# Expanded rows of the edge passes: three parts summed in one PSUM bank and copied by ScalarE, two banks for each edge layer

## The chip, the cores and the metric

The kernel runs on one core of one Trainium2 chip. The metric is the device time of one execution in microseconds. The program is one launch of about 330,000 instructions. TensorE writes to PSUM, which has eight banks of 512 f32 values in each of 128 partitions; `bank[0]` to `bank[7]` are these.

## The reference

Four graph networks run one after the other over the same 12,500 nodes (64 features) and 212,500 edges, which are sorted by destination. Between them stand a residual and a layer norm. The change touches the third, which has five layers:

```python
for l in range(5):
    h = leaky(x @ W1[l] + b1[l]) @ W2[l] + b2[l]
    e = leaky(edge_attr @ We1[l] + be1[l]) @ We2[l] + be2[l]     # 32 -> 64 -> 64, per edge
    msg = h[src] * e * dot_scale[l]
    agg = jax.ops.segment_sum(msg, dst, num_segments=n)
    x = layernorm(x + agg * res_w[l]) * ln_g[l] + ln_b[l]
```

## The kernel before

The hybrid pass does the edge part of one layer: `h[src] * e`, summed by destination. It runs five times, each with 271 *works*. A work is a batch of edges: tiles of 128 edges, one edge a partition. Two kinds alternate.

- A **near** work (147 a pass) has 7 tiles ("cells"). Its source rows are picked out of a table in SBUF by one-hot matmuls: `table_parts` holds every f32 row as three bf16 parts of 64 columns side by side (192 columns), and `hot_buf` holds the one-hot matrices in fp8, loaded by SP from DRAM, a chunk for each work. Seven near works make a strip. Its sums by destination come from one-hot matmuls too, into `bank[6]`, over the whole strip.
- A **far** work (124 a pass) has 8 tiles. Its source rows are gathered from DRAM by GpSimd, eight indirect DMAs a work (line 1133), up to four works ahead. Its one-hot matrices are made by VectorE (line 1275).

Both kinds have the two edge layers: the hidden layer (f32 matmuls of the edge attributes, line 1180, into `bank[4]`; ScalarE copies it to `hidden` with the bias, line 1145; VectorE does the leaky relu, line 1260), then the edge layer (a bias matmul, line 1188, and f32 matmuls, line 1192, into `bank[5]`). VectorE multiplies this with the source rows (lines 1285 and 1288). The product is split in three bf16 parts: ScalarE writes the high part (line 1150), VectorE takes it off (line 1313), ScalarE writes the middle part (line 1154), VectorE the low part (line 1318). TensorE adds up (lines 1217 near, 1225 far), VectorE reduces the three parts of the sum (lines 1325 and 1330) and adds them to `acc` (lines 1341 and 1350).

*Expansion before.* For a near work, `expand` runs 14 matmuls (7 cells, two sides) of 192 columns, line 1205, in two lots of four and three cells. Each lot goes to a pair of banks of a ring (`bank[0:2]`, `bank[2:4]`), 256 columns apart, and VectorE sums the three parts of each cell out of the pair into `cell_row` (`cell_sums`, line 1268). The far sums take a turn in the same ring. `s_free` counts what VectorE has emptied, and the numbers `op`, `ring`, `filled` and `added` of a work say which turn of the ring is its own.

*Order.* Each engine has its order written out as a `turn` per work, unrolled over 26 works inside a loop. Per work n, TensorE does: the hidden layer of n + 3, `expand` of n + 2 (if near), the edge layer of n + 2, `add_up` of n. VectorE does, one work ahead of TensorE (n its newest product): `take_sums` of n - 2, `multiply` of n, `cell_sums` part 0 or `one_hot` of n + 1, `rest_of_high` of n, `leaky` of n + 2, `cell_sums` part 1, `low_part` of n, `add_sums_of` n - 2. With one bank for each edge layer, the hidden layer waits until ScalarE has copied the one before, and the edge layer until VectorE has multiplied the one before.

## Time and profile before

| | us |
|---|---|
| median of 3 timed runs | 22706.24 (22622.63 to 22733.8) |
| the profiled execution | 22674.76 |
| its span, first to last instruction | 22672.7 |
| of that, the stretch with the five hybrid passes | about 10830 to 21170 |

The mean granted TensorE clock over the span is 0.735 of full speed. The page gives each engine's busy time; its groups say how often a line ran, how long one took and what ended the idle time ahead of it. "remote" there is a semaphore for which no instruction of the record ended at that moment; "issue" is time in which the engine waited for nothing that the profile shows. Matmul starts are those of issue, and their ends are modelled.

### The profile page before, as it was taken

The page shows a single profiled execution, that of the slowest core. Times are in us where ns is not written, and L with a number is a line of the kernel's source. Part 1 is how long each engine was busy: PE and PEld are TensorE (multiplying, and loading weights), DVE is VectorE, ACT ScalarE, POOL GpSimd, SP SyncE. Part 2 cuts the span into 40 slices and gives each one's busy share as a digit, 9 for nine tenths or more (in the row PEclk, how much of TensorE's full clock was granted, in tenths as well). Part 3 has the DMA queues.
Part 4 walks back from the last instruction along what each step waited for, and adds up shares of the span by engine and source line. Part 5 has one row for each costly group of instructions (what it writes and reads, how often), then busy time and mean ns, then how long its engine had stood idle before and what let it go on. Part 6 is the DMA issues. An engine that isn't in the chain of part 4 may idle for free. (4 is left out here: it accounts for less than half of the span.)

```text
span 22672.7 us, 329567 instructions
## 1 busy us (share of the span) xinstructions
PE 12966.2 (57%) x95507; PEld 10907.3 (48%) x95507; DVE 11406.3 (50%) x19693; ACT 5335.2 (24%) x10114; POOL 10006.5 (44%) x10482
## 2 busy tenths in 40 slices
PE   0344444556455666666566666666666666666465
PEld 0222223555345555555455555555555555555454
DVE  7544544444991121212555655565566556555413
ACT  0000000111443333333222222222222222222233
POOL 0455554665014434343455454445444544455342
PEclk9656665555557777778888887878887878778777
DMA  2111111111344434343222222222222222222343
GB/s 75 35 39 39 39 39 40 51 52 49 148 176 116 117 108 115 108 115 103 71 70 69 63 70 67 70 62 70 70 66 68 70 69 64 69 70 70 82 116 90
DMA packets 1284160, 1745.76 MB, mean 77 GB/s; under 512 B 576614, under 2 KB 828390, under 8 KB 1283174
## 3 DMA queue, kind: packets, MB, share of 16 engines
q1 hardware_dynamic: 960833, 1351.53, 19.9%
q0 software_dynamic: 317440, 348.12, 7.9%
q10 hardware_dynamic: 5040, 35.13, 0.4%
q8 instruction: 493, 8.08, 0.1%
q14 instruction: 354, 2.90, 0.0%
HBM read 1425.04 MB, written 308.76 MB: 76 GB/s over the span
## 5 line engine op out<-in xcount | busy, mean ns | idle before, releaser
L1133 POOL DMA_INDIRECT rows_buf<-feature_table,idx_buf x4960 | 4909.1, 990 | 4909.7 <-DMA idx_buf<-src_idx 3013.8
L857 POOL DMA_INDIRECT rows_buf<-feature_parts,idx_buf x2176 | 2054.4, 944 | 2878.2 <-PE banks L912 1897.8
L899 PE MATMUL banks<-sums_space,tmp 128*128 128x192 bf16 x13720 | 2090.6, 277 | 1602.1 <-issue 1109.7
L869 ACT ACTIVATE sums_space<-banks 128x384 bf16<-128x384 f32 x3920 | 1638.1, 452 | 3290.6 <-PE banks L886 2316.3
L886 PE MATMUL banks<-table_parts,tmp 128*128 128x192 bf16 x13720 | 2088.1, 276 | 299.5 <-DMA tmp<-one_hots 280.9
L899 PEld LDWEIGHTS banks<-sums_space,tmp 128*128 128x128 fp8e4 x13720 | 1333.0, 109 | 1869.2 <-issue 1831.8
L1180 PE MATMUL banks<-attr_buf,params 128*128 128x256 f32 x5420 | 1776.9, 454 | 782.9 <-ACT hidden L1145 354.6
L707 POOL DMA_INDIRECT rows_buf<-attention_table,idx_buf x1664 | 1571.9, 945 | 1455.7 <-DVE parts L1447 906.0
L1268 DVE TENSOR_REDUCE early<-banks 128x256 f32<-128x768 f32 (+1 forms) x1470 | 1253.6, 853 | 1861.9 <-remote 1482.3
L1150 ACT ACTIVATE sums_space<-onehot 128x448 bf16<-128x448 f32 (+1 forms) x1355 | 814.2, 601 | 5156.9 <-DVE onehot L1288 1442.6
L1192 PEld LDWEIGHTS banks<-params,hidden 128*128 128x128 f32 x10840 | 1768.0, 231 | 106.3 <-issue 39.0
L1192 PE MATMUL banks<-params,hidden 128*128 128x128 f32 x10840 | 1773.4, 316 | 30.0 <-issue 29.4
L1520 PE MATMUL banks<-far_ident,onehot 128*128 128x512 bf16 x1664 | 924.8, 556 | 1435.4 <-DVE red L1456 908.7
L1456 DVE TENSOR_REDUCE red<-banks 128x8 f32<-128x1024 f32 x832 | 1001.3, 1222 | 1460.8 <-remote 1194.9
L1188 PE MATMUL banks<-rest,parts 128*128 128x512 bf16 x1355 | 603.8, 446 | 1753.7 <-DVEq L1304 656.7
L1180 PEld LDWEIGHTS banks<-attr_buf,params 128*128 128x128 f32 x5420 | 1105.6, 226 | 1008.5 <-ACT hidden L1145 386.5
L886 PEld LDWEIGHTS banks<-table_parts,tmp 128*128 128x128 fp8e4 x13720 | 1412.4, 111 | 338.3 <-issue 298.4
L1205 PE MATMUL banks<-table_parts,tmp 128*128 128x192 bf16 x10290 | 1201.3, 271 | 609.1 <-issue 466.6
L1580 POOL DMA_INDIRECT edge_records<-hidden,idx_buf x1120 | 1120.6, 1001 | 717.1 <-ACT hidden L1623 378.9
L1205 PEld LDWEIGHTS banks<-table_parts,tmp 128*128 128x128 fp8e4 x10290 | 1002.3, 109 | 846.1 <-issue 733.9
L947 DVE TENSOR_REDUCE sums_space<-banks 128x64 f32<-128x192 f32 x272 | 97.2, 357 | 2575.3 <-PE banks L912 2368.8
L1217 PE MATMUL banks<-sums_space,tmp 128*128 128x192 bf16 x10290 | 1147.8, 262 | 327.0 <-issue 310.8
(380 smaller groups left out, 22377.4 us busy)
## 6 DMA issues: line engine op xcount, KB each, us to landing
tmp<-one_hots SPq DMA_DIRECT2D x1715, 448.0 KB
one_hots<-tmp SPq DMA_DIRECT2D x245, 448.0 KB
attr_buf<-attr SPq DMA_DIRECT2D x760, 128.0 KB
attr_buf<-cell_attr SPq DMA_DIRECT2D x735, 128.0 KB
rows_buf<-feature_table,idx_buf POOLq DMA_INDIRECT x4960
gathered_rows<-rows_buf SPq DMA_DIRECT2D x208, 272.0 KB
rows_buf<-gathered_rows SPq DMA_DIRECT2D x208, 272.0 KB
rows_buf<-feature_parts,idx_buf POOLq DMA_INDIRECT x2176
```

What stands on the lines that cost most here:

```text
L707: pool.indirect_dma_start(out=slot_rows(u, t), out_offset=None, in_=source, in_offset=bass.IndirectOffsetOnAxis(ap=idx_buf[:, u, t:t + 1], ...
L857: pool.indirect_dma_start(out=far_rows[:, u, t, :], out_offset=None, in_=table3, in_offset=bass.IndirectOffsetOnAxis(ap=idx_buf[:, u, t:t ...
L869: act.activation(cell_rows[:, q, 0:width], bank[q][:, 0:width], ACT.Copy).then_inc(s_cells_sb, 1)
L886: ins = pe.matmul(bank[q][:, j % 2 * 3 * D:(j % 2 + 1) * 3 * D], hot_buf[:, k, j, side * P:(side + 1) * P], table_parts[:, 2 * (k * CELLS ...
L899: ins = pe.matmul(bank[4 + h][:, half * 3 * D:(half + 1) * 3 * D], hot_buf[:, k, j, (2 + half) * P:(3 + half) * P], cell_rows[:, q, j % 2 ...
L1133: pool.indirect_dma_start(out=edge_rows[:, u, t, :], out_offset=None, in_=table, in_offset=bass.IndirectOffsetOnAxis(ap=idx_buf[:, u, t:t ...
L1180: ins = pe.matmul(bank[4][:, pair * 2 * P:(pair + 1) * 2 * P], w1[:, pair * P:(pair + 1) * P], attr_buf[:, w.attr, :, :].rearrange("p a e ...
L1192: ins = pe.matmul(bank[5][:, t * D:(t + 2) * D], hidden[:, w.side, at:at + P], w2, start=False, stop=(half == 1 and pair == 1))
L1205: ins = pe.matmul(to[:, j % 4 * 2 * P:j % 4 * 2 * P + 3 * D], hot_buf[:, w.k, j, side * P:(side + 1) * P], table_parts[:, 2 * (w.k * CELLS ...
L1217: ins = pe.matmul(bank[6][:, half * 3 * D:(half + 1) * 3 * D], hot_buf[:, w.k, j, (2 + half) * P:(3 + half) * P], sent[:, w.side, j, :], s ...
L1268: dve.tensor_reduce(out=cell_row[:, 4 * part:4 * part + cells, :], in_=pair_of_banks(w.ring + part).rearrange("p (j n) -> p j n", j=4)[:, ...
L1580: pool.indirect_dma_start(out=records, out_offset=bass.IndirectOffsetOnAxis(ap=idx_buf[:, slot, t:t + 1], axis=0), in_=record_buf[slot][:, ...
```

## The change

For a near work the expansion now writes one bank: each cell takes 64 columns of `bank[0]`, and its three parts are three matmuls of 64 columns that accumulate there, 42 matmuls for 14. ScalarE copies the 448 columns to `cell_row` in one instruction; VectorE's two reductions are gone. The ring of banks is gone too: far sums have `bank[1]`, the edge layer alternates between `bank[2]` and `bank[3]`, the hidden layer between `bank[4]` and `bank[5]`. TensorE and SP work one work further ahead with the hidden layer and its attributes, and TensorE expands before the hidden layer. VectorE multiplies first, and then takes and adds the sums of n - 2 in one go. Two semaphores, `s_row` and `s_taken`, stand for `s_free`.

```diff
 def hybrid_pass(block):
+            expanded, far_bank, strip_bank = bank[0], bank[1], bank[6]
+            def edge_bank(w):
+                return bank[2 + w.side]
+            def hidden_bank(w):
+                return bank[4 + w.side]
...
 @block.scalar
+                def copy_rows(w):
+                    act.wait_ge(s_fill, w.chunk + 1)
+                    if not w.begins:
+                        act.wait_ge(s_mult, w.n - (0 if w.follows_near else 1))
+                    act.activation(cell_row[:, 0:CELLS, :].rearrange("p t d -> p (t d)"), expanded[:, 0:CELLS * D], ACT.Copy).then_inc(s_row, 1)
-                def turn(w_next, w_ahead):
+                def turn(w_next, w_later, w_ahead):
                     if w_next:
                         high_part(w_next)
                     if w_ahead:
                         copy_hidden(w_ahead)
                     if w_next:
                         middle_part(w_next)
+                    if w_later and w_later.near:
+                        copy_rows(w_later)
...
 @block.tensor
                 def hidden_layer(w, early=False):
-                    if not w.begins:
-                        pe.wait_ge(s_act_hid, w.n)
+                    if not early:
+                        pe.wait_ge(s_act_hid, w.n - 1)
...
                 def edge_features(w, early=False):
-                    if not w.begins:
-                        pe.wait_ge(s_mult, w.n)
+                    if not early:
+                        pe.wait_ge(s_mult, w.n - 1)
...
                 def expand(w):
                     pe.wait_ge(s_chunk[w.k], w.s * 16 + 16)
                     pe.sem_inc(s_turn, 1)
-                    for part, cells in enumerate((range(0, 4), range(4, CELLS))):
-                        pe.wait_ge(s_free, w.op + (part + 1))
-                        pe.sem_inc(s_turn, 1)
-                        to = pair_of_banks(w.ring + part)
-                        for j in cells:
-                            for side in range(2):
-                                ins = pe.matmul(to[:, j % 4 * 2 * P:j % 4 * 2 * P + 3 * D], hot_buf[:, w.k, j, side * P:(side + 1) * P],
-                                                table_parts[:, 2 * (w.k * CELLS + j) + side, :], start=(side == 0), stop=(side == 1))
-                        ins.then_inc(s_fill, 1)
+                    pe.wait_ge(s_row, w.chunk + 1)
+                    pe.sem_inc(s_turn, 1)
+                    for j in range(CELLS):
+                        for side in range(2):
+                            for n in range(3):
+                                ins = pe.matmul(expanded[:, j * D:(j + 1) * D], hot_buf[:, w.k, j, side * P:(side + 1) * P],
+                                                table_parts[:, 2 * (w.k * CELLS + j) + side, n * D:(n + 1) * D],
+                                                start=(side == 0 and n == 0), stop=(side == 1 and n == 2))
+                    ins.then_inc(s_fill, 1)
...
-                def turn(w, w_later, w_ahead):
-                    if w_ahead:
-                        hidden_layer(w_ahead)
+                def turn(w, w_later, w_ahead, early=False):
                     if w_later and w_later.near:
                         expand(w_later)
+                    if w_ahead:
+                        hidden_layer(w_ahead, early and w_ahead.n < 2)
                     if w_later:
-                        edge_features(w_later)
+                        edge_features(w_later, early)
                     if w:
                         add_up(w)
...
-                        turn(work(i, pos), work(i, pos + 2), work(i, pos + 3))
+                        turn(work(i, pos), work(i, pos + 2), work(i, pos + 4))
...
 @block.vector
                 def turn(w_past, w_next, w_later, w_ahead):
+                    if w_next:
+                        multiply(w_next)
+                    if w_later and not w_later.near:
+                        one_hot(w_later)
                     if w_past:
                         take_sums(w_past)
-                    if w_next:
-                        multiply(w_next)
-                    if w_later and w_later.near:
-                        cell_sums(w_later, 0)
-                    elif w_later:
-                        one_hot(w_later)
+                        add_sums_of(w_past)
                     if w_next:
                         rest_of_high(w_next)
                     if w_ahead:
                         leaky(w_ahead)
-                    if w_later and w_later.near:
-                        cell_sums(w_later, 1)
                     if w_next:
                         low_part(w_next)
-                    if w_past:
-                        add_sums_of(w_past)
```

SP's `next_attributes` runs for the work four ahead instead of three. The waits of the sums (`s_free` with `op` and `ring`) become `s_taken` with the number of the far work, and the numbers `op`, `ring`, `filled` and `added` fall away.

## Rows read from the trace of the kernel before

**Rows 1.** The page: busy us (share) xinstructions of each engine.

```profile
PE 12966.2 (57%) x95507; PEld 10907.3 (48%) x95507; DVE 11406.3 (50%) x19693; ACT 5335.2 (24%) x10114; POOL 10006.5 (44%) x10482
```

**Rows 2.** Windows over the five hybrid passes: the first, and the sum.

```profile
core 0: us, PE busy (x) PEld busy (x) DVE busy (x) ACT busy (x) POOL busy (x), PEclk, DMA share, GB/s
...
10830.00:12852.00 2022.00, 1274.89 (x8879) 1077.99 (x8879) 1222.46 (x2199) 511.63 (x862) 1006.88 (x1010) 0.82 0.27 69
...
sum 10127.00, PE 6459.51 PEld 5469.49 DVE 6091.61 ACT 2556.43 POOL 5011.12; mean PE 1291.90 PEld 1093.90 DVE 1218.32 ACT 511.29 POOL 1002.22
```

**Rows 3.** Groups by shape in the first pass: busy us, mean ns, idle before.

```profile
L1133 POOL DMA_INDIRECT rows_buf<-feature_table,idx_buf x992 | 982.0, 990 | 977.1 <-DMA idx_buf<-src_idx 607.1 <-issue 283.9 <-DVEq L1312 86.2
...
L1205 PE MATMUL banks<-table_parts,tmp 128*128 128x192 bf16 x2058 | 238.1, 269 | 143.9 <-issue 104.9 <-DVE early L1330 38.0 <-DVE early L1268 0.9
...
L1205 PEld LDWEIGHTS banks<-table_parts,tmp 128*128 128x128 fp8e4 x2058 | 198.5, 108 | 190.6 <-issue 167.6
...
L1268 DVE TENSOR_REDUCE early<-banks 128x256 f32<-128x768 f32 x147 | 140.3, 954 | 338.8 <-remote 268.4 <-PE banks L1205 60.2 <-issue 8.7
...
L1268 DVE TENSOR_REDUCE early<-banks 128x192 f32<-128x576 f32 x147 | 110.4, 751 | 37.7 <-remote 37.6
...
L1313 DVE TENSOR_TENSOR onehot<-onehot,sums_space 128x448 f32<-128x448 f32 x147 | 90.8, 617 | 58.8 <-ACT sums_space L1150 33.0 <-issue 25.8
...
L1313 DVE TENSOR_TENSOR onehot<-onehot,sums_space 128x512 f32<-128x512 f32 x124 | 85.1, 686 | 1.0
```

**Rows 4.** Timeline without disturbance: start us, duration us, engine, line, operation.

```profile
12005.75 1.91 PE L1192 MATMUL banks<-params,hidden 128*128 128x128 f32 x8
...
12011.18 0.96 DVE L1268 TENSOR_REDUCE early<-banks 128x256 f32<-128x768 f32 x1 [1.16 <-PE banks L1205]
...
12018.78 1.32 PE L1205 MATMUL banks<-table_parts,tmp 128*128 128x192 bf16 x14
...
12019.70 0.95 DVE L1268 TENSOR_REDUCE early<-banks 128x256 f32<-128x768 f32 x1
...
12019.94 0.38 PE L1188 MATMUL banks<-rest,parts 128*128 128x512 bf16 x1
...
12020.16 1.05 PE L1192 MATMUL banks<-params,hidden 128*128 128x128 f32 x8
...
12021.05 1.32 PE L1217 MATMUL banks<-sums_space,tmp 128*128 128x192 bf16 x14
...
12022.20 1.06 PE L1180 MATMUL banks<-attr_buf,params 128*128 128x256 f32 x4
```

**Rows 5.** Windows, sums from 10880 to 12700: starved stretches (all, line 1313), then the rest.

```profile
sum 998.38, PE 529.22 PEld 433.18 DVE 412.48 ACT 175.09 POOL 644.93; mean PE 6.01 PEld 4.92 DVE 4.69 ACT 1.99 POOL 7.33
...
sum 998.38, DVE 60.37; mean DVE 0.69
...
sum 821.62, PE 626.71 PEld 544.60 DVE 677.60 ACT 279.12 POOL 278.91; mean PE 7.12 PEld 6.19 DVE 7.70 ACT 3.17 POOL 3.17
...
sum 821.62, DVE 103.89; mean DVE 1.18
```

**Rows 6.** Timeline of a starved stretch.

```profile
11024.77 0.82 PE L1225 MATMUL banks<-sums_space,onehot 128*128 128x192 bf16 x8
...
11032.73 0.36 DVE L1330 TENSOR_REDUCE early<-banks 128x64 f32<-128x192 f32 x1 [6.28 <-remote]
...
11040.38 0.10 PEld L1217 LDWEIGHTS banks<-sums_space,tmp 128*128 128x128 fp8e4 x1 [2.00 <-issue]
...
11041.08 0.32 PE L1217 MATMUL banks<-sums_space,tmp 128*128 128x192 bf16 x1 [1.16 <-issue]
```

**Rows 7.** Windows in the strip passes of another stage: starved, then free.

```profile
7308.41:7316.09 7.68, 1.98 (x19) 1.59 (x20) 0.00 (x0) 1.67 (x4) 4.46 (x5) 0.82 0.20 44
...
7316.09:7325.49 9.40, 8.91 (x83) 8.43 (x81) 0.93 (x3) 3.90 (x10) 3.07 (x4) 0.78 0.53 157
```

**Rows 8.** Timeline: narrow matmuls of an early stage.

```profile
3781.79 0.29 PEld L1734 LDWEIGHTS banks<-window_dst,tmp 128*128 128x128 bf16 x8 [1.38 <-ACT tmp L1600]
```

124 lines of the change are left out of this document (48 added, 76 removed).

## The prediction

> **What bounds the kernel now.** I read the page first [rows 1], then cut out the part that the diff touches. The five edge passes of the third network fill about 10,127 us [rows 2] of a span of 22,673: one pass is 2,022 to 2,060 us, 271 works long (147 near, 124 far), so 1,355 works in all. No engine is full in them: TensorE 64% busy, VectorE 60%, ScalarE 25%, GpSimd 49%. Such an average hides two regimes, and the timeline shows both.
>
> *The free regime.* From one reduction of expanded rows to the next such one, a near and a far work take 8.52 us [rows 4], and VectorE issues without a gap. TensorE is close behind. By distances between starts [rows 4]: expansion 1.16 us (12018.78 to 12019.94), edge layer 1.11 (to 12021.05), near sum 1.15 (to 12022.20), hidden layer 1.06, and for the far work the same for both layers and 0.82 for its sum [rows 6]: 7.5 us of the 8.52.
>
> *The starved regime.* In rows 6 the eight far matmuls are issued at 11024.77, with 0.82 us of work, but VectorE's reduction of their sum starts at 11032.73, after 6.28 us of idleness. Later TensorE issues single instructions 0.70 us apart: weight load 11040.38, matmul 11041.08. What goes on then is a run of GpSimd's gathers, eight DMAs per far work of 0.99 us each and 0.29 between them [rows 3]. I cut 1,820 us of the first pass by one rule: a starved stretch begins 4 us after a run of gathers starts and ends 2 us after its last one. The 88 starved stretches are 998 us with VectorE 41% busy; the rest is 822 us with 82% [rows 5]. Line 1313 runs once a work with a mean of (90.8 + 85.1)/271 = 0.649 us [rows 3], so 60.37/0.649 = 93 works fall in starved stretches and 103.89/0.649 = 160 in the others [rows 5]: **10.7 us a work starved, 5.13 us free**. The starved time is set by the gathers, 992 a pass, whatever the other engines do.
>
> *What limits TensorE in a starved stretch.* By the code the pairs of a load and a matmul are: near 14 + 9 + 14 + 4 = 41, far 9 + 8 + 4 = 21, so 41 x 147 + 21 x 124 = 8,631 in a pass and 31.8 a work (the 8,879 of rows 2 hold some of the stage behind the pass). 10.7/31.8 = 0.34 us a pair. The strip passes of another stage, quite another mix, give 7.68/20 = 0.38 us a pair in a starved stretch, and 9.40/83 = 0.11 right behind it [rows 7]. The same price for bf16 matmuls of 192 columns and for a mix with f32 ones, and 0.70 us for a load as for a matmul, say that the price goes by instruction and not by columns. That is the step on which this forecast rests.
>
> **The change, part by part.**
>
> *Expansion in 42 narrow matmuls for 14 wide.* Every wide one has a load of its own (2,058 of each [rows 3]), so I count 28 more pairs for a near work. A pass then has 8,631 + 28 x 147 = 12,747 pairs, 47.0 a work, 48% more. In the free regime a narrow pair may be cheap: the trace of before has no 64-column one, but eight of 24 columns with fresh loads issue in 0.29 us, 36 ns each [rows 8], and 192 columns take 1.16/14 = 83 ns [rows 4]. So the bounds are 1.5 us (36 ns) and 3.5 us (83 ns) for 42; I take 36 ns, as by columns 64 is nearer to 24. TensorE then has 7.5 - 1.16 + 1.5 = 7.8 us in a pair of works.
>
> The Trainium skill (TensorE: Matmul & The Clock Gate, Back-to-back issue gap) speaks against the split: it gives about 81 ns for each matmul in a stream of loads and matmuls at 128 columns, and says that below 64 columns an issue floor of about 25 ns takes over. By the first figure the expansion would be 3.4 us; row 8's 36 ns, at 24 columns, is nearer to the floor.
>
> *VectorE.* Its two reductions (954 and 751 ns, 147 times each a pass [rows 3]) go. At best that is 1.6 us off 8.52 us. One part returns: nothing stands any more between the multiplication of a far work and the wait for ScalarE's high part except the take and add of the sums, so I take 6.9 to 7.2 us. They drop below TensorE's 7.8.
>
> *ScalarE.* One copy of 448 columns out of PSUM, a near work. No such row exists; between nothing and 0.7 us, the nearest being its other calls (25% busy [rows 2]). It stands behind the middle part, and behind it wait the high part and the hidden copy of the next work. VectorE's low part of about 0.6 us covers it; if that cover were gone it would cost its whole 0.6 us a near work, 0.4 ms in all.
>
> *Two banks each, hidden layer one work earlier, far sums in their own bank, the multiplication ahead of the sums.* They remove waits between TensorE and VectorE. TensorE's edge layer no longer waits for the multiplication before it. I cost these at nothing beyond letting the pair of works come down to the busiest engine, 7.8 us. SP's attribute loads are issued one work further ahead and pass no other load that anyone waits for; index loads still stand behind the same two waits.
>
> *Fast works.* 7.8 for 8.52 us is a ratio of 0.915. Part of the free time is at the lower of the two clock levels (the mean granted clock is 0.82 [rows 2], and the edge layer's eight f32 pairs take 1.91 us at 12005.75 for 1.05 later [rows 4]); TensorE was the bound there already and nothing is gained, so I take 0.925: 5.13 x 0.925 = 4.75 us a work (bounds 4.4 and 5.13).
>
> **The sum.** 1,820 us held 253 works, 7.19 us each; 1,355 works are 9,744 us: 5,345 starved (498 works) and 4,399 free (857).
> (a) Slow time is fixed at 5,345 us, but a work costs 10.7 x 47.0/31.8 = 15.8 us in it: 338 works instead of 498. 1,017 works are left for the free regime at 4.75 us: 4,831. Sum 10,176, which is 432 us more.
> (b) A run of gathers bites only after some 4 us, as if TensorE lived from instructions in hand: 4/(5.13/31.8) = 25 pairs. With more pairs a work the same 25 last 25 x 4.75/47.0 = 2.5 us. The starved stretches, 88 x 9,744/1,820 = 471, would start 1.5 us earlier: 6,050 us starved with 383 works, 972 x 4.75 = 4,617 free, together 10,667: 923 us more.
> Between 432 and 923 I take 620. On the profiled execution's 22,675 us that is 23,295; the median of the timed runs lies 31 us above it, so 23,325; I round to 23,300.
>
> **The rivals.**
> 1. *Slow stretches go by columns or by the gathers' own traffic, not by instruction (faster).* Then 498 works still pass in them, and 857 free ones at 4.75 us are 4,071: 328 us less, about 22,380. For it: no wide and narrow pairs can be compared inside one starved stretch. Against it: 0.34 and 0.38 us for different mixes, 0.70 us for load and matmul alike. It decides when a work of 47.0 pairs costs under about 12.5 us in a starved stretch. With free works at 4.4 us it would reach 22,080.
> 2. *Narrow pairs aren't cheap.* At 83 ns the expansion is 3.5 us, TensorE needs 7.5 - 1.16 + 3.5 = 9.8 us a pair of works, a ratio of 1.15: 5.9 us a free work. 5,345 + 1,017 x 5.9 = 11,345, so 1,600 more: 24,300. Rows 8 speak against it, but eight pairs may be a burst from a full queue.
> 3. *The two effects cancel, or the three matmuls of one weight share a load.* Then only 28 instructions come on 64 to 82 of a near work instead of 56; starved works cost about 13.3 us, 402 of them, 953 x 4.75 = 4,527, sum 9,872: 128 more, 22,830, at the edge of what can be told. Against it: loads and matmuls are equal in number for this line [rows 3].
> 4. *VectorE gives nothing back* (free works stay at 5.13 us) with (b): 6,050 + 972 x 5.13 = 11,036, 1,290 more: 24,000.
>
> **How the numbers follow.** Forecast with its two bounds 0.47, rival 1 0.23, rival 2 0.08, rival 3 0.12, rival 4 0.10. The likeliest case's own range is 22,950 to 23,700. Cases of both signs hold most of the chance, so the range that should hold 8 in 10 reaches from rival 1's 22,380 to rival 4's 24,000, drawn in slightly at the top, where rivals 2 and 4 are thin. About 0.5% (115 us) is what a measurement of this kernel can tell from no change. Faster 0.24 (rival 1 and a little of 3), same 0.12, slower 0.64.
>
> **What would show it in the profile of after.** The groups of one pass: 42 x 147 = 6,174 matmuls of 64 columns with as many loads; no reduction of 256 or 192 rows; one new ScalarE copy, 147 times. Starts of narrow matmuls in an undisturbed expansion 25 to 40 ns apart (rival 2: about 80). Cut by the same rule, starved stretches should have about 15.8 us a work (rival 1: 10.7), the others 4.75. VectorE's share in free stretches should fall from 82% to under 75% and TensorE's rise. All other stages should keep their times. The forecast is wrong if starved works stay under 12.5 us, or if free ones fall below 4.4.

## The result, and the profile after

The kernel after takes 22,934.88 us, median of 4 runs (22,905.09 to 22,971.15); the kernel before, beside it, 22,664.44 (22,613.59 to 22,733.8). The ratio is 1.0118, 95% interval 1.0081 to 1.0154: 270 us slower. A second timing of the two gave 1.0086 (1.0064 to 1.0108), 200 us. The direction was forecast; the size was less than half of the 620 us forecast. The interval lies wholly above 1, so the change is a small loss and not noise.

The page of after, the line that answers to [rows 1]:

```profile
PE 13363.8 (58%) x116087; PEld 11096.2 (48%) x116087; DVE 10381.8 (45%) x18223; ACT 5664.6 (25%) x10849; POOL 10018.6 (44%) x10482
```

20,580 more pairs of a load and a matmul (28 x 735), 1,025 us less work on VectorE, 329 us more on ScalarE. Windows over the five hybrid passes of after, for [rows 2]; the columns are those of rows 2:

```profile
10830.00:12900.00 2070.00, 1377.67 (x12951) 1136.75 (x12951) 1010.75 (x1892) 573.75 (x1002) 1006.97 (x1007) 0.77 0.26 68
...
sum 10365.00, PE 6855.89 PEld 5651.03 DVE 5057.99 ACT 2870.33 POOL 5026.84; mean PE 1371.18 PEld 1130.21 DVE 1011.60 ACT 574.07 POOL 1005.37
```

The five stretches sum to 10,365 us for 10,127, and the spans differ by 230 (22,903.0 for 22,672.7): all of it lies here, and the other stages kept their times. Groups by shape of the first pass of after, for [rows 3]:

```profile
L1202 PE MATMUL banks<-table_parts,tmp 128*128 128x64 bf16 x6174 | 321.6, 200 | 478.3 <-issue 477.2
L1202 PEld LDWEIGHTS banks<-table_parts,tmp 128*128 128x128 fp8e4 x6174 | 251.8, 102 | 534.2 <-issue 533.1
...
L1186 PE MATMUL banks<-rest,parts 128*128 128x512 bf16 x271 | 122.7, 453 | 13.1 <-issue 7.3 <-DVE hidden L1257 5.3
...
L1300 DVE TENSOR_TENSOR onehot<-onehot,sums_space 128x448 f32<-128x448 f32 x147 | 91.5, 623 | 52.5 <-ACT sums_space L1140 33.9 <-issue 18.4
L1300 DVE TENSOR_TENSOR onehot<-onehot,sums_space 128x512 f32<-128x512 f32 x124 | 85.1, 686 | 0.9 <-issue 0.9
...
L1150 ACT ACTIVATE early<-banks 128x448 f32<-128x448 f32 x147 | 78.3, 533 | 565.8 <-remote 479.7 <-PE banks L1202 86.1
```

6,174 narrow pairs as counted, each with its load; ScalarE's copy is 533 ns; nearly all idle time ahead of the narrow matmuls is "issue" (477 of 478 us), where the engine waited for nothing that the profile shows. L1186 is the edge layer's bias matmul. Its row in the same view of before was not among those I had picked, and should have been:

```profile
L1188 PE MATMUL banks<-rest,parts 128*128 128x512 bf16 x271 | 118.4, 437 | 343.5 <-DVE onehot L1285 132.8 <-DVEq L1304 123.9 <-issue 60.3
```

TensorE stood idle 343.5 us of the pass ahead of this matmul; after, 13.1. VectorE's multiplication ended 132.8 us of it, and 123.9 more ended at line 1304, where VectorE raises the same semaphore for the first two works of a strip; 60.3 is "issue".

Timeline of after in an undisturbed stretch, for [rows 4]:

```profile
12012.91 1.35 PEld L1202 LDWEIGHTS banks<-table_parts,tmp 128*128 128x128 fp8e4 x42
12012.99 1.39 PE L1202 MATMUL banks<-table_parts,tmp 128*128 128x64 bf16 x42
...
12014.21 1.11 PE L1178 MATMUL banks<-attr_buf,params 128*128 128x256 f32 x4
...
12015.89 0.52 ACT L1150 ACTIVATE early<-banks 128x448 f32<-128x448 f32 x1
```

42 narrow matmuls in 1.39 us, 33 ns each (forecast 36); the hidden layer starts 1.22 us behind the first of them, and ScalarE's copy is 0.52 us. The Trainium skill (TensorE: Matmul & The Clock Gate, Back-to-back issue gap) puts an issue floor of about 25 ns at 64 columns and below; this row lies near that, and far from its 81 ns for 128 columns.

The starved stretches of the first pass by the rule of the prediction, and the rest, for [rows 5]; first all instructions, then line 1300:

```profile
sum 991.62, PE 442.94 PEld 304.69 DVE 277.31 ACT 148.56 POOL 658.98; mean PE 6.24 PEld 4.29 DVE 3.91 ACT 2.09 POOL 9.28
...
sum 991.62, DVE 50.04; mean DVE 0.70
...
sum 828.38, PE 776.74 PEld 698.52 DVE 592.34 ACT 350.52 POOL 238.29; mean PE 10.79 PEld 9.70 DVE 8.23 ACT 4.87 POOL 3.31
...
sum 828.38, DVE 109.72; mean DVE 1.52
```

Line 1300 takes (91.5 + 85.1)/271 = 0.652 us a work, so 76.8 works in 992 starved us (12.9 us each) and 168.4 in 828 (4.92). The starved time is unchanged (998 before); VectorE's share in the free stretches fell from 82% to 72%, TensorE's rose from 76% to 94%.

From here on I count over all five passes: each start of this subtraction of VectorE (1,355 of them) is one work, and it is starved if it falls between 4 us after the start and 2 us after the end of a run of at least seven gathers (no pause of 1.2 us or more between them). Free time is the rest, less the four gaps between passes. Rates counted so are per execution; they depend on where the rule puts its edges, so they compare kernels and are not durations of anything.

```
kernel                    starved us  works  us/work | free us  works  us/work
before                       5,319     471    11.3   |  4,479    884    5.07
before, second profile       5,355     490    10.9   |  4,409    865    5.10
after                        5,480     391    14.0   |  4,534    964    4.70
after, second profile        5,507     394    14.0   |  4,525    961    4.71
```

The second profiles are those of *before_again* and *after_again* below, on another machine.

### The profile page after: what moved, and what is told of

The parts are those of the page before. It is cut to its first block and busy times, and to the rows that moved or that the text cites. A ratio compares the mean times of both kernels' runs of the same rounds, so it can differ in the third digit from the quotient of the medians.

```text
span 22903.0 us, 368412 instructions
## 1 busy us (share of the span) xinstructions
PE 13363.8 (58%) x116087; PEld 11096.2 (48%) x116087; DVE 10381.8 (45%) x18223; ACT 5664.6 (25%) x10849; POOL 10018.6 (44%) x10482
## 5 line engine op out<-in xcount | busy, mean ns | idle before, releaser
L1202 PE MATMUL banks<-table_parts,tmp 128*128 128x64 bf16 x30870 | 1600.7, 200 | 2450.0 <-issue 2439.0
L1202 PEld LDWEIGHTS banks<-table_parts,tmp 128*128 128x128 fp8e4 x30870 | 1258.3, 102 | 2734.8 <-issue 2729.2
L887 PE MATMUL banks<-table_parts,tmp 128*128 128x192 bf16 x13720 | 2095.5, 277 | 302.9 <-DMA tmp<-one_hots 280.8
L900 PEld LDWEIGHTS banks<-sums_space,tmp 128*128 128x128 fp8e4 x13720 | 1335.1, 109 | 1874.1 <-issue 1837.1
L1178 PE MATMUL banks<-attr_buf,params 128*128 128x256 f32 x5420 | 1904.9, 473 | 385.7 <-issue 201.4
L1272 DVE TENSOR_TENSOR onehot<-banks,early 128x448 f32<-128x448 f32 x735 | 456.4, 621 | 3420.7 <-PE banks L1190 1657.1
L887 PEld LDWEIGHTS banks<-table_parts,tmp 128*128 128x128 fp8e4 x13720 | 1418.0, 111 | 338.6 <-issue 297.5
L1215 PEld LDWEIGHTS banks<-sums_space,tmp 128*128 128x128 fp8e4 x10290 | 979.9, 107 | 437.5 <-issue 407.5
```

The costliest lines, as they stand in the source:

```text
L887: ins = pe.matmul(bank[q][:, j % 2 * 3 * D:(j % 2 + 1) * 3 * D], hot_buf[:, k, j, side * P:(side + 1) * P], table_parts[:, 2 * (k * CELLS ...
L900: ins = pe.matmul(bank[4 + h][:, half * 3 * D:(half + 1) * 3 * D], hot_buf[:, k, j, (2 + half) * P:(3 + half) * P], cell_rows[:, q, j % 2 ...
L1178: ins = pe.matmul(hidden_bank(w)[:, pair * 2 * P:(pair + 1) * 2 * P], w1[:, pair * P:(pair + 1) * P], attr_buf[:, w.attr, :, :].rearrange( ...
L1202: ins = pe.matmul(expanded[:, j * D:(j + 1) * D], hot_buf[:, w.k, j, side * P:(side + 1) * P], table_parts[:, 2 * (w.k * CELLS + j) + side ...
L1215: ins = pe.matmul(strip_bank[:, half * 3 * D:(half + 1) * 3 * D], hot_buf[:, w.k, j, (2 + half) * P:(3 + half) * P], sent[:, w.side, j, :] ...
```

## The experiments

The six lots of runs fell on machines of two kinds. In three of them, and in the timing above, the kernel before took 22,632 to 23,153 us, with starved stretches as in the trace that I had read. In the three others it took 16,224 us: GpSimd's gathers run on end, and nothing is starved. One chip number came up with both kinds, so I can't say whether it is the chip or something beside it. Ratios are always to the kernel before on the same machine; each lot says of which kind it was. The forecast is for the first kind. Works and prices counted in a trace hold for its machine: on that of the first lot, where the kernel before takes 2% more, no trace of it was taken.

### The expansion's instructions and columns (first kind, before 23,153 us)

*a1_wide*: 14 wide matmuls in the kernel after, written over one another in the one bank, so the near rows are not summed.

```diff
+                        to = expanded[:, j % 3 * 2 * D:(j % 3 * 2 + 3) * D]
                         for side in range(2):
-                            for n in range(3):
-                                ins = pe.matmul(expanded[:, j * D:(j + 1) * D], hot_buf[:, w.k, j, side * P:(side + 1) * P],
-                                                table_parts[:, 2 * (w.k * CELLS + j) + side, n * D:(n + 1) * D],
-                                                start=(side == 0 and n == 0), stop=(side == 1 and n == 2))
+                            ins = pe.matmul(to, hot_buf[:, w.k, j, side * P:(side + 1) * P],
+                                            table_parts[:, 2 * (w.k * CELLS + j) + side, :],
+                                            start=(side == 0), stop=(side == 1), skip_group_check=True)
```

> The kernel after with the expansion in 14 matmuls of 192 columns again, all written into the one bank (cells overlap there, so the expanded rows are not summed: that part of the computation is left out). Everything else of the change stays. It has the columns of the kernel after and 31.8 pairs of a load and a matmul a work for 47.0. My theory, mended by the result: the work in a starved stretch pays by the pair, 10.7 us at 31.8 pairs and 12.9 at 47.0; so 10.7 us again, 500 of 1,355 works in 5,350 us of starved time, and 855 at about 4.8 us: 9,450 us for the five passes for about 10,050, so near 22,330. Rival, columns or the gathers' own traffic decide and not the pairs: within 100 us of the kernel after, 22,930. Rival, another part of the change (the order, the waits) makes it slower: 22,900 too, and the starved work stays at 12.9 us.

*a2_third*: `for n in range(1)`, so 14 matmuls of 64 columns; the middle and low parts are left out.

> The kernel after with only the high part of the three expanded: 14 matmuls of 64 columns (the middle and low parts of the source rows of near works are left out). The pairs are those of the wide form, the columns a third of them. If pairs set the price of a starved stretch, it is like the wide form there (10.7 us a work) and at best 0.3 us a free work quicker: 22,150 to 22,330. If columns set it, it must gain clearly on the wide form in starved stretches (under 10 us a work), and lie under 22,000.

*a4_five*: `n` over 0, 1, 2, 0, 1, so 70 matmuls of 64 columns; two parts are added twice.

> The kernel after with 70 matmuls of 64 columns in the expansion for 42: the high and middle parts are added twice (so the near source rows are changed in value). 62.2 pairs a work. By the pair with the slope of before to after (0.145 us a pair): 15.1 us a starved work, 354 works in 5,350 us, 1,001 free ones at 5.1 us: 10,455 us for the passes, about 400 more than the kernel after, 23,340. If the price per pair grows in proportion instead (0.274 us each): 17 us a starved work and 23,500. If pairs don't matter: only the free works pay, about 100 us, 23,030.

*b1_narrow*: the split alone, in the kernel before.

```diff
-                                ins = pe.matmul(to[:, j % 4 * 2 * P:j % 4 * 2 * P + 3 * D], hot_buf[:, w.k, j, side * P:(side + 1) * P],
-                                                table_parts[:, 2 * (w.k * CELLS + j) + side, :], start=(side == 0), stop=(side == 1))
+                                for n in range(3):
+                                    at = j % 4 * 2 * P + n * D
+                                    ins = pe.matmul(to[:, at:at + D], hot_buf[:, w.k, j, side * P:(side + 1) * P],
+                                                    table_parts[:, 2 * (w.k * CELLS + j) + side, n * D:(n + 1) * D],
+                                                    start=(side == 0 and n == 0), stop=(side == 1), skip_group_check=True)
```

> The kernel before with this part of the change alone: its 14 expanding matmuls of 192 columns are 42 of 64, into the same places of the same ring, so that VectorE's two reductions, the banks and the order stay. My theory: 12.9 us a starved work for 10.7, 414 works in 5,345 us; the free works stay at 5.13 us, as VectorE sets them: 10,172 us for 9,744, so 430 more, 23,090. If the price of the split is less than the two kernels together show, and other parts of the change cost something, it is under 22,900. If pairs don't matter: 22,660 as before.

```
kernel       us       ratio (95%)              starved works, us/work | free us/work
a1_wide    22,600  0.9758 (0.9735 to 0.9780)     424  13.0           |  4.26
a2_third   22,603  0.9763 (0.9741 to 0.9786)     429  13.0           |  4.22
a4_five    24,427  1.0553 (1.0527 to 1.0578)     314  17.1           |  5.54
b1_narrow  24,024  1.0378 (1.0352 to 1.0404)     276  19.2           |  5.12
```

The kernel with a third of the columns is equal to the one with all of them, 22,603 for 22,600: the expansion's columns cost nothing, and rival 1, as far as it speaks of them, is out. (A load and its matmul came and went together in all these runs, so they don't say which of the two is paid for.) Groups of the expansion in the first pass of a1_wide, and of b1_narrow:

```profile
L1202 PE MATMUL banks<-table_parts,tmp 128*128 128x192 bf16 x2058 | 250.5, 272 | 136.7 <-issue 129.4 <-ACT early L1150 6.6
```

```profile
L1207 PE MATMUL banks<-table_parts,tmp 128*128 128x64 bf16 x6171 | 318.7, 205 | 390.1 <-issue 373.1 <-DVE early L1333 14.5 <-DVE early L1271 0.8
...
L1188 PE MATMUL banks<-rest,parts 128*128 128x512 bf16 x271 | 123.5, 456 | 212.2 <-DVEq L1307 83.4 <-issue 67.1 <-DVE onehot L1288 58.8
```

The idle time ahead of the expansion goes with the instructions: 129 us of "issue" for 2,058 wide ones, 373 and 477 for 6,171 and 6,174 narrow. a1_wide lies 3.6% under after by the ratios (0.9758 to 1.0118), some 820 us where I expected 600. The split alone costs the kernel before 3.78%, twice what I expected of this run; its free works keep their price (5.12 for 5.07 to 5.10), and some 200 fewer works pass in starved time than in the two profiles of before, from other machines. And the rest of the change, without the split, is worth -2.42%. The two sum to +1.4%, against 1.18% and 0.86% measured. a4_five shows that the mended form had the price too small as well: 4.3% over after, 990 us, for the 400 expected. In time of the first machine (22,664 us) 42 to 70 instructions cost 990 to 1,060 us, 14 to 42 cost 740 to 820.

The prices of a starved work missed what I expected as well: 13.0 us in a1_wide and a2_third for 10.7, 19.2 in b1_narrow for 12.9. Over the pairs of a work (31.8, 47.0, 62.2) the table gives 0.41 us a pair in a1_wide, 0.41 in b1_narrow and 0.27 in a4_five, so the starved work has no fixed price by the pair.

What a run of gathers does shows best by the time since its start. Weight loads that start in a microsecond, mean over all runs of exactly 16 gathers (the sixteenth starts after some 19 us), and how many have started after 8 and after 20 us; the last two kernels are of a later lot:

```
us since the first gather   0-2   4-6   6-8  8-10 10-12 12-14 14-16 16-18 18-20 22-24 | to 8  to 20
before, second profile      8.3   7.7   5.5   3.2   2.4   2.7   2.7   1.9   1.2   2.3 |   54     82
b1_narrow                   8.2  10.0   7.2   2.5   2.2   1.9   1.3   1.2   0.9   3.7 |   62     82
a1_wide                     8.3   9.3   5.0   2.5   1.9   1.4   1.1   1.1   0.9   3.3 |   62     80
a2_third                    8.5   9.5   3.8   1.9   2.0   1.4   1.2   1.0   0.9   3.8 |   63     80
after, second profile       8.4   9.6   3.0   2.0   1.9   1.8   1.7   1.4   1.2   3.9 |   65     85
a4_five                     9.2  11.5   2.0   1.2   1.8   1.3   1.3   1.0   0.9  10.0 |   65     80
a7_one_edge                 8.9  11.3   2.8   1.8   2.0   1.6   1.5   1.2   1.0   3.6 |   66     84
b5_two_edge                 8.4   6.8   4.1   4.4   5.3   4.8   3.1   1.9   1.0   2.2 |   55     96
```

From the eighth microsecond on TensorE starts 1 to 3 loads a microsecond in the first seven kernels, whatever the width and whatever the mix: [rows 6] had shown it once, a load and its matmul 0.70 us apart. The last column is the plainest: in the first 20 us of a run TensorE starts 80 to 85 pairs, with 31.8, 47.0 or 62.2 pairs to a work. That is a price by the instruction, as a number of pairs for a run of gathers. A kernel that goes quickly at first has fewer left for the rest. In runs of 8 gathers the number is less even, 57 to 60 by the end of the run in before, b1_narrow, a1_wide and a2_third and 69 to 72 in after, a4_five and a7_one_edge. b5_two_edge is the exception, with 4 to 5 a microsecond up to the fourteenth and 96 in all, at the pairs of before; why isn't known.

### The gathers taken away (first kind, before 22,632 us)

*before_again* and *after_again* are the two kernels unchanged. *b2_no_gather* and *a3_no_gather* have this edit in the hybrid pass:

```diff
-                        for t in range(G):
-                            pool.indirect_dma_start(out=edge_rows[:, u, t, :], ...).then_inc(s_rows[u], 16)
+                        pool.memset(edge_rows[:, u, :, :], 0.0).then_inc(s_rows[u], 1)
```

The waits for `s_rows` are changed to this count; the far rows are zero.

> The kernel before, unchanged, for its profile on the chip of these runs. The four runs ahead of this one were made on a chip on which the kernel before takes 23,150 us, 2% more than the 22,664 beside which the kernel after was first timed. Expected: the extra 490 us lie partly ahead of the passes (the passes of the runs so far on that chip begin 217 us later), partly in starved stretches, where a work should take over 11.3 us (over all five passes it is 11.29 on the first chip).

> The kernel after, unchanged, on the chip of these runs. 1.2% over the kernel before, as on the first chip, so about 23,430. By the runs of the parts it should be the sum of the rest of the change (the kernel with 14 wide matmuls: 550 us under the kernel before) and of the split (870 us as a change alone in the kernel before): 320 us more than before. If the split costs less on top of the other parts, it is under 23,300.

> The kernel before with the eight gathers of each far work in the five passes replaced by one GpSimd memset of its rows (so the source rows of far works are zero; the index loads stay). No starved stretch is left in the passes. All 1,355 works go at the free price of before, 5.1 us: 6,900 us and 540 between the passes, for 10,330 to 10,600, so 20,000 to 20,300. If something else than the gathers starves TensorE, more than 21,500.

> The kernel after with the same edit (far source rows zero). The free price of after is 4.7 us: 6,370 and 540, so 500 to 570 us less than the same edit gives in the kernel before, near 19,700. So the sign of the change turns when the gathers go. If the split costs time in free stretches too, the two are level; if the split's cost has nothing to do with the gathers, this kernel stays 1% over the other.

```
kernel           us       ratio (95%)              five passes us | us/work
before_again   22,593   one run                        10,291
after_again    22,834   1.0086 (1.0064 to 1.0108)      10,569
b2_no_gather   19,093   0.8435 (0.8418 to 0.8453)       6,783     |  4.62
a3_no_gather   18,171   0.8027 (0.8009 to 0.8044)       5,862     |  3.94
```

The machine was not the one of the first lot, so its extra 490 us weren't seen in the kernel before. But outside the five passes the kernels of the first lot take 12,569 to 12,607 us, and the others of this kind 12,299 to 12,357, so about half of the 490 us lies outside the passes. Without gathers the sign turns, as expected, but by 922 us where I had 500 to 570. The gathers cost before 3,508 us and after 4,707, 1,199 more. Windows over the first pass without gathers, from its first to its last work, b2 and then a3:

```profile
10837.94:12089.36 1251.42, 1010.76 (x8573) 902.17 (x8571) 1143.20 (x2070) 480.02 (x808) 63.03 (x120) 0.97 0.28 81
```

```profile
10802.55:11872.79 1070.24, 1005.86 (x12624) 925.28 (x12621) 941.86 (x1778) 543.60 (x954) 63.05 (x120) 0.97 0.33 96
```

The pass of b2, 1,251 us, has VectorE busy 1,143 of them (91%) and TensorE 1,011. The pass of a3, 1,070 us, has TensorE busy 1,006 (94%) and VectorE 942. So the busiest engine changes, as forecast, and TensorE's 7.8 us a pair of works is right (2 x 3.94 = 7.88). What I had wrong is the pace before: I read 8.52 us off one near and one far work [rows 4]; without gathers it is 2 x 4.62 = 9.24. That pair holds none of the strips' work on VectorE (lines 1299, 1307, 1325 and 1341 of before, some 58 us a pass, 0.2 us a work), nor any wait. The granted clock is 0.97 of full speed in both, so these two say nothing on the discount that I took for the lower clock level.

### One part of the rest at a time (second kind, before 16,224 us)

*a5_one_edge*: one edge bank in the kernel after.

```diff
             def edge_bank(w):
-                return bank[2 + w.side]
+                return bank[2]
...
-                    if not early:
-                        pe.wait_ge(s_mult, w.n - 1)
+                    if not w.begins:
+                        pe.wait_ge(s_mult, w.n)
```

*b4_two_edge*: a second edge bank in the kernel before.

```diff
-                        pe.wait_ge(s_mult, w.n)
-                    pe.matmul(bank[5], ones_bf, ...)
+                        pe.wait_ge(s_mult, w.n - 1)
+                    pe.matmul(bank[5 + 2 * w.side], ones_bf, ...)
...
-                        group_hot[:, w.slot, :, :], bank[7][:, 0:P]. ...
+                        group_hot[:, w.slot, :, :], iota1[:, :]. ...
```

*a6_wide_no_gather* and *b3_narrow_no_gather* are a1_wide and b1_narrow with the edit of the lot before.

> The kernel after with one bank for the edge layer, and TensorE's wait for the multiplication of the work before, as in the kernel before; all else as in after. In the kernel before, the edge layer's bias matmul sat 343.5 us idle in the first pass, in after 13.1, and without gathers the free work is 0.68 us cheaper in after (4.33 us, gaps between passes included, for 5.01). My theory now: this one wait is that gain, which I had costed at nothing beyond 7.8 us a pair of works. Then this kernel loses about 0.6 us on each of 960 free works: 450 to 600 us over after, near 23,400. Rival: VectorE's relief (its two reductions gone) is the gain, and the second edge bank adds nothing to it: within 100 us of after.

> The kernel before with a second bank for the edge layer alone: it alternates between banks 5 and 7, TensorE waits for the multiplication two works back, and the one-hot matrices of far works read their numbers from SBUF, where bank 7 held them. Wide expansion, ring, VectorE's reductions and order stay. VectorE is 90% busy in the kernel before without gathers, so it bounds the gain: 4.26 us (half of 8.52) for about 4.6 a free work. If the wait is what the change took away: 300 to 500 us under before, 22,150 to 22,350. If VectorE's relief is needed for any gain: within 100 us of before.

> The kernel after without the gathers of the five passes (one GpSimd memset of the rows instead; far source rows zero) and with the 14 wide matmuls written over one another into one bank (near source rows not summed). Beside the kernel after without gathers (18,171) it gives the price of the split where nothing starves. TensorE is 91% busy there: 42 narrow take about 0.2 us more than 14 wide in 735 expansions, so this one is 100 to 200 us below, 18,000. If the split's 820 us have nothing to do with the gathers, it is near 17,400.

> The kernel before without the gathers (far source rows zero) and with its 14 wide matmuls as 42 narrow. With the gathers this split cost 3.8%. Without them: 19,093 plus nothing to 200 us, as the two reductions and the wait of the edge layer bound the work, not TensorE. If the split costs the same 870 us here, gathers are not its cause.

```
kernel                us       ratio (95%)              five passes us
a5_one_edge         16,181   0.9972 (0.9962 to 0.9983)       7,091
b4_two_edge         16,770   1.0335 (1.0317 to 1.0352)       7,680
a6_wide_no_gather   14,899   0.9182 (0.9166 to 0.9197)       5,808
b3_narrow_no_gather 15,852   0.9770 (0.9753 to 0.9786)       6,773
```

The total times can't be set beside those of the other kind. The passes without gathers can, with care, since nothing in them is starved on either: 6,773 us narrow for 6,783 wide in the kernel before, 5,862 narrow for 5,808 wide in after (6,783 and 5,862 are from the first kind). So without gathers the split costs nothing in before and 54 us in after, and nearly all of its 3.8% is the gathers' doing.

The first two missed their question: all passes there last as long as GpSimd's gathers. Groups of the first pass of b4_two_edge:

```profile
L1133 POOL DMA_INDIRECT rows_buf<-feature_table,idx_buf x992 | 1114.1, 1123 | 346.7 <-issue 294.3 <-DMA idx_buf<-src_idx 46.6 <-DVEq L1312 5.8
...
L1275 DVE TENSOR_TENSOR onehot<-iota,rows_buf 128x1024 bf16<-128x1024 f32 x124 | 151.2, 1219 | 0.3
```

The gathers fill the pass (1,114 us and 294 of issue between them, of a pass of some 1,430). They take 1,123 ns where they take 1,007 in the kernel after on such a machine (below): 4,960 x 0.116 = 575 us, and 546 were lost. VectorE's one-hot comparison, which now reads two operands from SBUF, does it. Over the five passes of b4 the gathers that overlap this comparison by more than 0.2 us take 1,843 ns on average and those that don't touch it 983; in the kernel after, where one operand comes from PSUM, 964 and 1,024. A second edge bank by itself doesn't lengthen them: 1,010 ns over the five passes of a5 with one bank, 1,009 in after with two. The Trainium skill (SBUF — State Buffer, Who interferes with whom) says that a `tensor_tensor` with both inputs in SBUF contends with GpSimd's reads of it, and the trace agrees. The same passage infers that descriptor generation isn't held up by it; these gathers were.

### The same two again (first kind, before 22,652 us)

*a7_one_edge* is a5_one_edge, *b5_two_edge* is b4_two_edge.

> The kernel after with one bank for the edge layer and TensorE's wait for the multiplication of the work before: the same kernel as a5_one_edge, for a chip on which the gathers starve TensorE. If the wait is the gain: 450 to 600 us over after, 1.9% to 2.6% on top of its 0.9% to 1.2%, so a ratio of 1.028 to 1.038. If VectorE's relief is the gain: 1.005 to 1.015. On a chip like the last, where the kernel before takes 16,200 us: 0.997 again.

> The kernel before with a second edge bank alone, the same kernel as b4_two_edge. A side effect showed there: with the one-hot numbers read from SBUF a gather took 1,127 ns for 1,010, and the passes were 3.3% longer for it. Where the gathers starve TensorE that adds up to 116 us a pass of starved time, 580 in all, of which works done in it give some back. The wait gone gives 300 to 500 us. So a ratio of 0.985 to 1.01; and TensorE's idle time before the bias matmul must fall from 343 us a pass to under 50 if the bank does what it should. If it falls and the free works don't get cheaper than 5.06 us, VectorE bounds them and not this wait.

```
kernel         us       ratio (95%)              starved us, works, us/work | free us/work
a7_one_edge  23,122   1.0211 (1.0190 to 1.0232)   5,473   375   14.6       |  4.90
b5_two_edge  22,280   0.9850 (0.9821 to 0.9878)   5,834   629    9.3       |  4.88
```

The bias matmul's row in the first pass of a7 (257 of its 271), then of b5:

```profile
L1186 PE MATMUL banks<-rest,parts 128*128 128x512 bf16 x257 | 116.8, 455 | 86.2 <-DVEq L1291 59.8 <-DVE onehot L1272 13.1 <-issue 12.7
```

```profile
L1188 PE MATMUL banks<-rest,parts 128*128 128x512 bf16 x271 | 117.2, 433 | 18.1 <-DVE hidden L1260 11.2 <-issue 6.2
```

The bank does what it should, 343.5 to 18.1 us. Added to before it is worth 1.5% (1.2% to 1.8%; 372 us), although the gathers are longer there too (1,040 ns for 990 [rows 3]); taken from after it costs 0.9% to 1.25% (1.0211 against 1.0118 and 1.0086), 210 to 280 us, about half of the 450 to 600 that I expected. So my second theory, that this one wait is the whole gain over before, was half right: the edge bank is a real part of the gain, and something else in the change, VectorE's relief or the second hidden bank or the order, another. b5 gains mostly in starved time (9.3 us a work, 629 works for 471 to 490); a reason for that, say that VectorE has a finished edge layer at hand when TensorE resumes, is a guess. With full results this kernel beats both before and after.

### The place of the multiplication, and plain loads (second kind, before 16,223 us)

*b6_multiply_first* is b5 with the multiplication ahead of the taking of the sums:

```diff
+                    if w_next:
+                        multiply(w_next)
                     if w_past:
                         take_sums(w_past)
-                    if w_next:
-                        multiply(w_next)
```

*d1_plain_loads*, in the kernel after:

```diff
-                            pool.indirect_dma_start(out=edge_rows[:, u, t, :], ..., in_=table, ...)
+                            pool.dma_start(edge_rows[:, u, t, :], table[t * P:(t + 1) * P, :])
```

> The kernel before with the second edge bank (as b5) and VectorE's multiplication ahead of the taking of the sums, as the change has it. In the second edge bank's run the reduction of far sums still had 170 us idle ahead of it in 1,700 us, and the multiplication, ready by then, stood behind it. If the place of the multiplication is the missing part of the 2.4%: a ratio of 0.975 to 0.982. If the missing part is VectorE's relief or the second hidden bank: 0.983 to 0.988, as the second edge bank alone (0.985).

> The kernel after with each of the 4,960 gathers of the five passes replaced by a plain DMA of the same size from GpSimd's queue (128 rows of 256 bytes, always the first 1,024 rows of the table, so the far source rows are not the right ones). If the bytes and descriptors of the gathers starve TensorE, starved stretches remain: over 22,000. If it is GpSimd's indirect DMAs (0.99 us of its time each), they go: 18,200 to 18,600, near the kernel after without gathers (18,171).

b6: 16,714 us, 1.0305 (1.0287 to 1.0322), 0.3% under b4 on the same kind of machine; its own question, for starved passes, wasn't answered. d1: 14,978 us, 0.9232 (0.9217 to 0.9248). A plain DMA is 535 ns of GpSimd's time there, and the passes take 5,889 us, 27 more than a3_no_gather's without any on the other kind of machine: bytes cost next to nothing here (always the same 1,024 rows, so not quite the gathers' traffic), and GpSimd's time does. That says nothing of what starves TensorE on the other kind.

### The last two (second kind, before 16,224 us)

*d2_plain_loads* is d1, *after_third* the kernel after.

> The kernel after with each gather of the five passes replaced by a plain DMA of the same size from GpSimd's queue (far source rows are not the right ones), as d1. On a chip where the gathers starve TensorE: over 22,000 if the bytes do it, 18,200 to 18,600 if GpSimd's indirect DMAs (0.99 us of its time each, 535 ns for a plain one in d1) do. On a chip like d1's: 14,980 again.

> The kernel after, unchanged. On a chip where the gathers starve TensorE: 0.9% to 1.2% over before, as measured twice. On a chip like d1's, GpSimd's gathers run on end and set the pace of the passes in both kernels (992 a pass at 1.01 us and 0.30 between them), so within 0.5% of before: 16,150 to 16,230.

d2: 14,976 us, 0.9235 (0.9219 to 0.9250), as d1. after_third: 16,185 us, 0.9976 (0.9966 to 0.9986): on this kind of machine the change is worth 40 us. Groups of its first pass:

```profile
L1122 POOL DMA_INDIRECT rows_buf<-feature_table,idx_buf x992 | 999.2, 1007 | 346.4 <-issue 298.0 <-DMA idx_buf<-src_idx 44.7 <-DVEq L1299 3.7
```

999 us of gathers and 298 of issue between them are 1,297 of the pass's 1,311 us. With TensorE and VectorE both waiting for GpSimd, neither the split nor the second bank shows.

## Why the prediction was right in direction and wrong in size

**What bounds the kernel now: right in kind.** Two regimes, the starved time nearly fixed by the gathers (5,319 us before, 5,480 after), and inside it a price by the instruction and not by columns: shown by a1 and a2, equal at a third of the columns, and by the 80 to 85 pairs in 20 us, but for b5. What comes nearest to fixed is the number of pairs in a run of 16. The 0.34 us a pair is no price of one: it was the mean over a stretch that begins at 7.7 loads a microsecond in before and ends at 1.2.

**The split: right, and mostly in size.** Term (a) with the free works left at 5.13 us is 5,345 + 1,017 x 5.13 = 10,562, 818 us over the 9,744 of before. The split alone measured 3.78%, 857 us of 22,664. Its terms agree less: 276 starved works at 19.2 us for 338 at 15.8. Where nothing starves a narrow pair is 33 ns, forecast 36, and the split moves the passes by -10 and +54 us. Rival 2 is out.

**The rest of the change: this step failed.** "I cost these at nothing beyond letting the pair of works come down to the busiest engine, 7.8 us." With "5.13 x 0.925 = 4.75 us a work" that made 1,017 x 0.38 = 386 us of gain; a1_wide measures 2.42%, 548 us. Two things were too small. First, the pace of before came from the best pair of the timeline, 8.52 us, and is 9.24 without gathers; VectorE's work for the strips was left out. 7.8 for 9.24 is a ratio of 0.84, and a1_wide's free works have it, 4.26 for 5.07 to 5.10, with no discount for the clock. Second, the wait of the edge layer, 343.5 us a pass in a row that I hadn't picked, has its own price where works stop and start: 372 us in the kernel before, 210 to 280 in after. How the remainder divides between VectorE's relief, the second hidden bank and the order stays open.

**The price of a starved work: this step failed too.** "A work costs 10.7 x 47.0/31.8 = 15.8 us in it": 14.0 was counted, and 391 works pass in starved time where I had 338. 53 works more at 4.75 us are 250 us of the forecast that did not come. The price does not go in proportion to the pairs, and I had let the rest of the change act on free works only. It acts on both: a1_wide, with the pairs of before, is at 13.0 us and not 11, and the split on top takes it to 14.0; alone, in before, the split takes it from 11 to 19, and the second bank alone from 11 to 9 (b5). Why they combine so is open.

**The free works: right by luck.** 4.70 for 4.75 us, but from two errors that cancel. The rest of the change alone gives 4.26, and the split adds the difference, though it costs nothing where no gather runs. The traces say where, though they are of two machines: from 2 to 6 us behind the last gather of a run, which the rule calls free, a work takes 6.4 to 6.7 us in after and 4.0 in a1_wide; beyond 6 us 4.2 in after and 4.5 in a1_wide. So part of the price of starvation lies behind the rule's edge; that TensorE makes up there what it is behind is my reading.

**The onset, (b): not borne out in size.** I took 188 us of it (620 - 432). Behind the start of a run the loads do thin out earlier in after than in before (3.0 for 5.5 in the seventh and eighth microsecond), but b1_narrow, which has as many pairs, is at 7.2. What the table does show is a number: in the first seven kernels the rate has fallen or falls when 54 to 66 loads have started, not 25. The starved time grew by 161 us, as runs of 16 gathers became more (121 to 193 in the second profiles) and runs of 8 fewer (281 to 136), not by the 705 of (b).

**The sum.** Forecast: 818 - 386 + 188 = 620. Measured: 857 - 548 = 309 for the two parts one by one, and 200 to 270 together, so they help each other by 40 to 110 us. In the trace: 5,480 + 4,534 = 10,014 us for 5,319 + 4,479 = 9,798, 216 more, for the 9,744 and 10,364 of the forecast. Of the 404 us between 620 and 216, 188 are the onset, 162 the passes of after (135 us more starved and 297 less free than in (a)) and 54 those of before (9,798 for 9,744).

**The rivals.** Rival 1 is out: columns cost nothing, the gathers' traffic is the same in b1_narrow, which lost 3.78%, and a starved work is over its 12.5 us. Rival 3's figure, 22,830, is near the result. Its first words, that the two effects cancel, come nearest to what happened, 857 us against 548; its working does not, since every narrow matmul has its own load. Rival 4 is out, VectorE fell from 60% to 49% of the passes and the free work from 5.1 to 4.7.

**Not settled:** what it is in a gather that starves TensorE, and why it does so on some machines alone. The plain loads met a machine without starving both times. A fixed number of pairs for a run looks like a supply of instructions that is cut off, but no run tests it, and the packets that bring instructions don't show it: the same 957 in the passes of after on both kinds of machine, 863 ns each on the first and 833 on the second. The price of a step from 42 to 70 instructions, higher than from 14 to 42, isn't explained either.

## What to carry to other kernels

Where one engine's instructions come at a trickle while another's DMAs run, count instructions and not columns: the same work in 42 for 14 matmuls cost 3.8%, and narrowing 14 matmuls to a third gained nothing. When a trace is cut into two regimes by a rule, look at the microseconds on both sides of its edges before a mean over one regime is used as a price: here it was part of a transient. Before a change that touches several engines is costed, list each wait of the profile that it removes with its idle time over a whole pass, and take an engine's pace from its busy time over the pass, not from the best pair of the timeline. A part worth taking alone may stand beside one that isn't: the second edge bank gave -1.5%, the split +3.8%.

## What the hardware showed beyond this

Machines of two kinds run the same kernel in 22,630 to 23,150 and in 16,224 us; on the second the starved stretches are missing, and this change, +0.9% to +1.2% on the first, is -0.2% there, while the second edge bank, -1.5% on the first, is +3.3%. VectorE's one-hot comparison reading its numbers from SBUF and not from PSUM keeps its own time (1,219 ns for 1,217) and makes the gathers of GpSimd 116 ns longer on average (1,123 for 1,007), and the lengthening lies on those that it overlaps (1,843 ns for 983).

On the first kind TensorE starts 80 to 85 pairs of a load and a matmul in the first 20 us of a run of 16 gathers, in seven of eight kernels of quite different pace; the eighth has 96.
